# Loading the attention output for the output projection: one DMA for all 16 heads against 16 DMAs of one head each

## The reference

```python
xn = (x - mu) * rsqrt(var + 1e-5) * ln_scale + ln_bias
xg = concatenate([g, xn], axis=1)                 # 16 global tokens in front
Q, K, V = [(xg @ W.T).reshape(B, G + T, 16, 128) for W in (Wq, Wk, Wv)]
scores = einsum('bqhd,bkhd->bhqk', Q, K) * scale + mask   # window 256 + global tokens
out = einsum('bhqk,bkhd->bqhd', softmax(scores), V).reshape(B, G + T, D)
attn = out[:, G:] @ Wo.T + x                      # the output projection
x = layernorm(x + attn)
gate, up = silu(qlinear(x, wq_gate)), qlinear(x, wq_up)   # 8-bit codes, 2048 -> 5632
x = layernorm(x + qlinear(gate * up, wq_down))            # 5632 -> 2048
```

## Time and profile before

| | |
|---|---|
| time of the runs shown | 5107.46 and 5363.93 us, median 5235.69 us |
| the profiled execution | 5116.9 us |
| its span, slowest core (core 4) | 5115.4 us (cores: 5085.8 to 5115.4 us) |
| PE busy | 3832.6 us, 75% |
| DVE busy | 1342.4 us, 26% |
| mean granted TensorE clock, core 4 | 0.906 |
| stage 3, core 4 | 1651 to 2217 us from the start of the span |

### The profile page before, as it was taken

How to read it: one execution, slowest core, us unless ns; L and a number is a source line. 1 busy time by engine, 2 the same in 40 slices (tenths; PEclk the granted TensorE clock), 3 DMA queues, 4 the chain that set the end, 5 groups by cost and what they waited for, 6 DMA issues and landing times.

```text
span 5115.4 us, 44479 instructions; the slowest of 8 cores (5085.8 to 5115.4 us)
## 1 busy us (share of the span) xinstructions
PE 3832.6 (75%) x16072; PEld 1450.9 (28%) x16072; DVE 1342.4 (26%) x1936; ACT 402.9 (8%) x661; POOL 316.4 (6%) x601
## 2 busy tenths in 40 slices
PE   2288998988987445459999986656799999766640
PEld 1133332323332122223333332212233333222210
DVE  6624434344344222231111110000122221000013
ACT  0001212121112000000000000000011110000000
POOL 0000000000000000000000001111000000111110
PEclk9999898999998677769999999989999999999985
DMA  2211102102011522233333334333444443234333
GB/s 82 68 24 27 30 13 42 21 16 40 13 24 22 107 82 82 82 78 66 62 63 66 66 67 74 50 60 57 82 114 116 116 99 63 31 58 59 59 86 156
DMA packets 203560, 322.63 MB, mean 63 GB/s; under 512 B 100292, under 2 KB 145349, under 8 KB 192597
## 3 DMA queue, kind: packets, MB, share of 16 engines
q0 software_dynamic: 85856, 180.46, 21.9%
q1 hardware_dynamic: 117494, 139.33, 8.4%
HBM read 437.23 MB, written 58.72 MB: 97 GB/s over the span
## 4 chain that ended last, share of the span: by engine, by line
PE 65%; DMA 16%; DVE 10%; issue 5%; ACT 1%; SPq 1%; DVEq 0%; POOL 0%; ACTq 0%; another core or an unknown queue 0%; POOLq 0%
PE p_gu L902 25%; DMA wdTt<-wd 10%; PE p_wo L708 5%; PE p_sc L458 4%; PE p_sc L470 4%; PE p_sc L506 4%; PE p_gu L1012 3%; PE p_gu L905 2%; PE p_srow L1210 2%; DMA aott<-aosp 2%; PE p_pv L1208 2%; DVE statst L296 2%; PE p_sc L552 2%; PE p_s L1012 2%; DVE xnfmt L362 2%
## 5 line engine op out<-in xcount | busy, mean ns | idle before, releaser
L902 PE MATMUL p_gu<-xn2ht,wgTt 128*128 128x512 bf16 x2816 | 642.6, 381 | 8.4 <-DVE rowLt L864 8.4
L902 PE MATMUL p_gu<-xn2ht,wuTt 128*128 128x512 bf16 x2816 | 638.4, 380 | 0.0
L708 PE MATMUL p_wo<-woTt,aott 128*128 128x512 bf16 x1024 | 265.1, 427 | 295.3 <-DMA aott<-aosp 249.8
L1012 PE MATMUL p_cs<-wdTt,hmidt 128*128 128x512 bf16 x352 | 138.9, 395 | 419.6 <-DMA wdTt<-wd 316.6
L933 DVE TENSOR_SCALAR gust<-p_gu,sutt 128x512 f32<-128x512 f32 x176 | 132.1, 750 | 1103.6 <-PE p_gu L907 1102.4
L1012 PE MATMUL p_gu<-wdTt,hmidt 128*128 128x512 bf16 x1408 | 381.2, 395 | 0.0
L902 PEld LDWEIGHTS p_gu<-xn2ht,wgTt 128*128 128x128 bf16 x2816 | 262.2, 98 | 377.2 <-issue 88.9
L902 PEld LDWEIGHTS p_gu<-xn2ht,wuTt 128*128 128x128 bf16 x2816 | 261.1, 98 | 365.5 <-issue 74.7
L571 ACT ACTIVATE p_sbt<-p_sc 128x512 bf16<-128x512 f32 x352 | 203.3, 596 | 1027.3 <-PE p_sc L555 1027.3
L1039 DVE TENSOR_TENSOR v2spt<-p_cs,sd_bct 128x512 f32<-128x512 f32 x8 | 5.5, 692 | 1018.2 <-PE p_cs L1021 1018.2
L923 ACT ACTIVATE gust<-p_gu,sgtt 128x512 f32<-128x512 f32 x176 | 121.0, 687 | 1848.0 <-PE p_gu L907 1834.3
(11 more groups left out here) (121 smaller groups left out, 2993.0 us busy)
## 6 DMA issues: line engine op xcount, KB each, us to landing
wgTt<-wg POOLq DMA_DIRECT2D x88, 512.0 KB, 6.3
wuTt<-wu POOLq DMA_DIRECT2D x88, 512.0 KB, 8.4
wdTt<-wd POOLq DMA_DIRECT2D x352, 128.0 KB, 2.9
xtilet<-x SPq DMA_DIRECT2D x16, 1024.0 KB, 5.4
xrest<-x SPq DMA_DIRECT2D x16, 1024.0 KB, 9.1
r2sp<-v1ht SPq DMA_DIRECT2D x16, 1024.0 KB, 5.1
v2sp<-v2spt SPq DMA_DIRECT2D x64, 256.0 KB, 2.1
v2at<-v2sp SPq DMA_DIRECT2D x16, 1024.0 KB, 5.5
```

What stands on the lines that cost most here:

```text
L708: ins = t.matmul(bank.p[:, :], aot[:, abuf * D + hc * 128:abuf * D + (hc + 1) * 128], woT[:, off + hc * 512:off + (hc + 1) * 512], start=( ...
L902: t.matmul(bank.p[:, :], wsl[:, j * D + dc * 128:j * D + (dc + 1) * 128], xn2h[:, dc * 1024 + tc * 512:dc * 1024 + (tc + 1) * 512], start= ...
L1012: ins = t.matmul(pd_banks[ti].p[:, :], hmid[:, hb * 1024 + ti * 128:hb * 1024 + (ti + 1) * 128], wdT[:, j * 512:(j + 1) * 512], start=(hb ...
```

## The change

The one DMA at L693 that loads all 16 heads of a token tile becomes a loop over the heads: 16 DMAs of one head each, with the same destinations, the same source bytes and the same semaphore. Each adds 16 to the semaphore `s_aot[abuf]`, so a tile's load adds 256 where it added 16, and PE's wait for the tile (`t_aotld[tt]`, the semaphore's count behind the last DMA) asks for all 16. Nothing else in the program changes.

```diff
             def f(sync, tt=tt, abuf=abuf):
                 wt(sync, t_womm.get(tt - 2))
-                src_ = ao_dram[tt].rearrange("h p k -> p h k")
-                dstv = aot[:, abuf * D:(abuf + 1) * D].rearrange(
-                    "p (h k) -> p h k", h=NH)
-                s_aot[abuf].inc(sync.dma_start(out=dstv, in_=src_), 16)
+                for h in range(NH):
+                    s_aot[abuf].inc(sync.dma_start(
+                        out=aot[:, abuf * D + h * 128:abuf * D + (h + 1) * 128],
+                        in_=ao_dram[tt, h]), 16)
             blk.sync(f)
             t_aotld[tt] = s_aot[abuf].tok
```

## The result

The changed kernel is slower by 0.9%: the ratio of its time to that of the kernel before is 1.0086, with a 95% interval of 1.0049 to 1.0123. On the profiled execution's 5116.9 us this is +44 us, 25 to 63 us; forecast were +26 us (5143 us, ratio 1.0051). The direction was right, and 5116.9 x 1.0086 = 5161 us lies inside the range of 5103 to 5195; the size was too small. The profiled execution after took 5175.7 us, the spans of its cores lie between 5139.8 and 5174.2 us.

The account below looks back on a forecast made before the run. Stage 3's engines take turns, with PE waiting for each load. Issue 7.05 us plus landing 1.8 us gives 8.85 us against 7.1, +1.75 us in 15 tiles, +26 us on 5116.9: 5143 us, range 5103 to 5195.

Parts of the forecast that it names:

- The load is on the path, 15 times: Stage 3: every tile but the first waits about 7.1 us for its load, together 106.5 us, 2.1%.
- 8.85 forecast: Stage 3 load per tile: 7.05 us to the last issue plus 1.8 us landing, +1.75 us per tile.
- the 16th piece is issued 15 x 0.47 = 7.05 us after the first: SP's issue in stage 3: 15 steps of 0.47 us each, bounds 5.55 and 7.5 us.
- rival A: Stage 3: the spill blocks SP's issue of pieces for 2.9 us, +70 us, 5187 us; chance 18%.
- the sheer number of rows outstanding: SP's queue in stage 3: rows outstanding block issues; 6 pieces have 768, well below 2048.
- Costed at nothing: Stage 3: first tile's load, residual's later issue, PE's clock and PE's wait for a higher count add no time.
- B: Stage 3 load: each piece starts only after the completion before, +206 us, 5322 us; chance 5%.
- C: Stage 3 load: one-head pieces interleave better, faster or no change, 5102 to 5113 us; chance 11%.
- SP would keep room for the residual's load: Stage 3: residual's load, issued behind all pieces, lands at 1875.7, needed by L739 at 1882.83; 7 us of cover left.
- the likeliest case: Stage 3 load paced by SP's issue: 5113 to 5159 us, most likely 5143; chance 66%.

Follow-up runs that it names:

- the two-queue run: Changed kernel's 16 pieces with even heads issued by SP and odd heads by ScalarE's queue: 33.1 to 33.3 us per tile on cores 0 to 3.

## Why the prediction was right or wrong

**The load is on the path, 15 times, and the issue would pace it: right.** The steps of 0.475 us, the landing of 1.7 to 2.3 us (core 0), the residual's short issue and the idle DMA engines between the pieces all came as written, and the clock costs 0.1 us per tile at most. With the spill out of the way the load measured 8.80 us against 8.85 forecast, and the two-queue run shows that most of the cost is the pace of the issuing engine and not the number of DMAs.

**The step that failed: "the 16th piece is issued 15 x 0.47 = 7.05 us after the first".** It is 8.21 us. The term left out was rival A in small: issues are held while the spill drains, but only pieces 2 and 3 feel it, with 0.5 and 0.6 us. I had rival A as all or nothing, with 2.9 us of hold, and against it two arguments that did not carry. One was the row in which 2048 rows were handed over in 0.39 us: that issue began 0.42 us after the spill's, and the hold begins at 0.8 us. The other was that "the sheer number of rows outstanding" blocks: piece 2 was held when one piece of 128 rows stood behind the spill. The 4.07 us of the residual's issue, which began 0.89 us after the spill's, against 0.99 us without a spill, was the warning, though it does not give the size. With 8.21 + 1.9 = 10.1 the sum would have been 5116.9 + 15 x 3.0 = 5162 us, against 5161 measured. That this agrees to 1 us is luck: it leaves out the first tile's 5 us and the last 0.3 us per tile, and the measured change is known only as 25 to 63 us.

**Costed at nothing, and wrong: the first tile.** "its PE waits for the output weights, up to 28.4 us at a time, far longer than 9 us" took for granted that the pieces would land in 9 us beside the weights' load. They landed 48 to 61 us after the first issue, near its end, which costs about 5.2 us. The earlier trace rows had the warning: even the single DMA took 9.2 us there on core 4 against 4.2 us on core 2.

**The rest of the period, 0.2 to 0.3 us per tile,** is the difference between the 3.27 us of the periods and the 3.0 us of the load as summed here. By the means, last pieces that land later than 1.9 us have 0.2 of it, and the first group of matmuls 0.1.

**The rivals.** A: there, at 1.1 of its 2.9 us. B (pieces one after another, 5322 us): refuted, the whole load takes 10.2 us and not 20.8, and the last piece no longer than 3.0 us. C (faster, or no change): refuted for 16 pieces by the measured interval; eight pieces come nearest to no change. That SP would keep room for the residual's load was right in this order (L739 still does not wait), and became wrong as soon as the periods were shorter.

**The bounds.** 5113 to 5159 for the likeliest case missed the 5161 by 2 us, because the hold was not part of it; the range, which took in rival A, held it.

## What to carry to other kernels

Cutting one DMA into n on the same engine costs (n - 1) issue steps before the last data start, and can pay back only where the consumer starts on the first pieces; here PE waited for all 16, and letting it start on the first was not tried. Before costing a burst of small DMAs at its bare step, look at what is moving at the time: here a 1024 KB spill held the issues that began 0.8 to 1.9 us after its own, on either engine's queue, and beside GpSimd's load of the weights single issues took up to 4.4 us. And where a load is on the path at all, first ask why it is issued so late: moving it ahead of the spill gained 3.45 us per tile, as much as the cutting cost, and issuing it a tile early 3.2% of the kernel, more than three times as much. Off the path is not for good either: where the other waits were gone and the period could be 15.5 us, a load of 12 us behind the spill was on it again.

## What the runs showed of the hardware that I had not expected

- An issue of a DMA over 64 partitions (16 KB) took SP 0.60 us, one over 128 partitions (32 KB) 0.43 us, each in a row of its kind. Why the smaller one is dearer stays open.
- One spill of 1024 KB issued just ahead adds about 3 us to the landing of a 512 KB load (7.1 against 4.0 us), and 1.2 us to the issue of 16 small ones (8.2 against 7.0 us).
- That hold is not bound to the queue of the spill: ScalarE's issues beside it took 1.0 and 1.1 us too, instead of 0.45.
- While GpSimd's weights were loading, SP's small issues took up to 4.4 us (3.7 on core 0) and a 32 KB piece landed up to 38.6 us after its issue; one 512 KB DMA issued just ahead of the same weights landed in 4.1 to 9.3 us in the kernel before, in 12.2 us at most in another run.
